# Level 64 of a triangular inverse: the z projection ahead of its first product, and its transposes and two products on 64x64 blocks of TensorE

## The chip, the cores and the metric

The kernel runs on one core of one Trainium2 chip. A core has TensorE (matrix products, "PE"; its weight loads "PEld"), VectorE ("DVE"), ScalarE ("ACT"), GpSimd ("POOL") and SyncE ("SP", which issues the DMAs here). The metric is the device time of one execution in microseconds; lower is better. All data are 32-bit floats. The engines run on their own instruction streams and wait for one another by semaphores.

## What is computed

The program is two transformer layers on x of shape (2, 1024, 256). Each layer adds an attention part and a feed-forward part to x. The change touches only the attention part of the first layer, a gated delta rule with 16 key heads, 32 value heads and head size 128. Cut to what matters:

```python
qkvz = hidden_states @ W_qkvz            # per key head: q, k, two v, two z
...
y = silu(conv4(mixed))                   # causal convolution over time, 4 taps
q = l2norm(q) * DK ** -0.5 ; k = l2norm(k)
def step(S, inp):                        # one token
    qt, kt, vt, gt, bt = inp
    S = S * exp(gt)[:, None, None]
    kv = einsum('hk,hkv->hv', kt, S)
    delta = (vt - kv) * bt[:, None]
    S = S + kt[:, :, None] * delta[:, None, :]
    return S, einsum('hk,hkv->hv', qt, S)
...
gated = core * silu(z)
gated = gated * rsqrt(mean(gated * gated) + EPS) * norm_w
return gated.reshape(B, Tn, VDIM) @ W_out
```

## The kernel before, in words

The tokens are handled in chunks of 128. Within a chunk the recurrence turns into matrix products with the inverse T of a unit triangular 128x128 matrix that is built from N (the decayed products of the keys); W is T transposed. One step of the long loop is one chunk of one key head, for both batches and both value heads, so each operation has U = 4 matrices side by side. There are 16 heads x 8 chunks = 128 steps (`STEPS`). The loop is a software pipeline: `body(s)` of every engine runs its functions on steps of different lag (`S_P`, `S_S`, `S_F`, `S_L`, `S_D`, `S_E` = 0, 1, 2, 5, 6, 7 steps back). The order of work on an engine is the order of the calls in its `body`; nothing reorders it. It is written out 16 times and looped (`pipeline`).

T is built in levels. GpSimd inverts the 16x16 blocks of the diagonal by rows (`base_first`, `base_rest`: once for two chunks, so that every second step has more GpSimd work), and SyncE carries them through DRAM into `Tm` and `Wm` (`base_out`, `dump`). TensorE and VectorE then join the blocks to 64x64 (`x16`, `w1`, `w2`, `w3` on TensorE; `xev16` and `add_k` on VectorE). The last level, 64, joins the two 64x64 halves:

- `t64` (L572): four transposes of W give T; `tev64` (ScalarE, L869) copies their upper left quarters from bank 5 to `Tm`.
- `x64` (L583): four products of N by the left half of T, into bank 5; `xev64` (ScalarE, L878) copies them negated to `Xs64`, whose right half stays zero.
- `w64` (L593): four products of `Xs64` by the right half of W into bank 4; `add_w64` (VectorE, L941) copies the upper 64 partitions into the upper right quarter of W. `solve` (L681) uses W in the next step.

All three are issued as 128-row products, though only one 64x64 quarter of each matters. A 32-bit product of one matrix shows as two matmul records, a transpose as one.

Around them stand in a step of TensorE: `state_in` (L513), `x16` (L528), `front` (L606, L611, L617), `solve` (L681), `w1` (L541), `apply` (L692, L695), `values` (L630), `w2` (L551), `project` (L651), `w3` (L561), `project` (L651), `t64`, `gated_tp` (L706: transposes of the gated output), `x64`, `zproj` (L668: x by the z weights, into bank 1), `w64`, `project_out` (L721: into bank 0). ScalarE copies gated_tp's result (`gtev`, L888) between `tev64` and `xev64`. VectorE's `accumulate` (L950) adds project_out's result to x. A tile's shape on the array follows from rows x columns of the weights; the profile writes it as 128*128.

Of the kernel before, what the change touches and what calls it, by code (L numbers as in the profile page):

```python
# [8 lines left out]
ACT = mybir.ActivationFunctionType  # L9
AX = mybir.AxisListType  # L10

P = 128
B, T, D = 2, 1024, 256
# [5 lines left out]
U = 4  # L19
# [89 lines left out]
def delta_rule(nc, ins, m, acc, xn, xnT, gates):  # L109
# [5 lines left out]
    RING = 4  # L115

    with ExitStack() as ctx:
# [30 lines left out]
        mkX = sb("mkX", [P, P])  # L148
        Xs = sb("Xs", [P, U, P])
        Wk = [sb(f"Wk{r}", [P, U, P]) for r in range(2)]  # L150
        Xs64 = sb("Xs64", [P, U, P])
        S = sb("S", [P, U, P])
        R = sb("R", [P, U, P])
        Us = sb("Us", [P, U, P])
# [72 lines left out]
        def wait(eng, sem, val):  # L227
            if not (isinstance(val, int) and val <= 0):
                eng.wait_ge(sem, val)
# [13 lines left out]
        with nc.Block() as block:  # L243
# [93 lines left out]
            @block.gpsimd  # L337
            def _(pool):
                pool.memset(conv[0][:], 0.0).then_inc(setup, 1)
                for tile in (S, Xs64):  # L340
                    pool.memset(tile[:], 0.0)
                pool.memset(mhalf[:], -0.5)
                pool.memset(mkX[:], -1.0)
                pool.wait_ge(m["made"], 2)
# [155 lines left out]
            def _(pe):  # L500
# [63 lines left out]
                def t64(s):  # L564

                    t = s.back(S_L)
                    if not t.live:
                        return
                    W = Wm[t.c // 2 % 2][:, t.c % 2]
                    wait(pe, w3_rdy, t.done())  # L570
                    for u in range(U):
                        i = pe.transpose(bU[5][:, u], W[:, u, :], m["ident"][:])  # L572
                    i.then_inc(t64_tp, 1)

                def x64(s):

                    t = s.back(S_L)
                    if not t.live:
                        return
                    T = Tm[t.c // 2 % 2][:, t.c % 2]  # L580
                    wait(pe, t64_rdy, t.done())
                    for u in range(U):
                        i = pe.matmul(bH[5][:, u], N[t.c % RING][:, u, :], T[:, u, 0:64], start=True, stop=True)  # L583
                    i.then_inc(x64_mm, 1)

                def w64(s):
                    t = s.back(S_L)
                    if not t.live:
                        return
                    W = Wm[t.c // 2 % 2][:, t.c % 2]  # L590
                    wait(pe, xs64_rdy, t.done())
                    for u in range(U):
                        i = pe.matmul(bH[4][:, u], Xs64[:, u, :], W[:, u, 64:], start=True, stop=True)  # L593
                    i.then_inc(w64_mm, 1)

                def front(s):
# [59 lines left out]
                def zproj(s):  # L656

                    t = s.back(S_L)
                    if not t.live:
                        return  # L660
                    pe.wait_ge(wz_in, t.head(16, 16))
                    wait(pe, araw_rdy, min(t.done(-S_L), STEPS) if t.i is None else t.done(-S_L))
                    ends(pe, s, exp_rdy, t, S_F - S_L)
                    ends(pe, s, zz_rdy, t, 1)
                    for b in range(B):
                        for k in range(KT):
                            n = 2 * t.c + b
                            i = pe.matmul(bB[1][:, b], xnT[:, k, n * P:(n + 1) * P], wz[:, k, :],  # L668
                                          start=(k == 0), stop=(k == KT - 1))
                    i.then_inc(z_mm, 1)  # L670
# [27 lines left out]
                def gated_tp(s):  # L698

                    t = s.back(S_E)  # L700
                    if not t.live:
                        return
                    pe.wait_ge(gatn_rdy, t.done())
                    wait(pe, o_rdy, min(t.done(-1), STEPS) if t.i is None else t.done(-1))
                    for u in range(U):
                        i = pe.transpose(bU[6][:, u], gatn[:, u, :], m["ident"][:])  # L706
                    i.then_inc(g_tp, 1)

                def project_out(s):

                    t = s.back(S_E)
                    if not t.live:
                        return
                    pe.wait_ge(gT_rdy, t.done())
                    wait(pe, wo_in, t.head(16, 16))
                    wait(pe, braw_rdy, min(t.done(-S_E), STEPS) if t.i is None else t.done(-S_E))
                    ends(pe, s, vb_rdy, t, S_F - S_E)
                    ends(pe, s, acc_rdy, t, 1)
                    for h in range(2):
                        for v in range(2):  # L720
                            i = pe.matmul(bB[0][:, h], gT[:, 2 * h + v, :], wout[:, v, :], start=(v == 0), stop=(v == 1))  # L721
                    i.then_inc(out_mm, 1)
# [15 lines left out]
                def body(s):  # L738
                    state_in(s)
                    x16(s)  # L740
                    front(s)
                    solve(s)
                    w1(s)
                    apply(s)
                    values(s)
                    w2(s)
                    project(s, 0)
                    w3(s)
                    project(s, 1)
                    t64(s)  # L750
                    gated_tp(s)
                    x64(s)
                    zproj(s)
                    w64(s)
                    project_out(s)
                    norm_tp(s)
                pipeline(pe, body)

# [1 line left out]
            def _(act):  # L760
# [102 lines left out]
                def tev64(s):  # L863

                    t = s.back(S_L)
                    if not t.live:
                        return
                    act.wait_ge(t64_tp, t.done())
                    act.activation(Tm[t.c // 2 % 2][0:64, t.c % 2, :, 0:64], bU[5][0:64, :, 0:64],  # L869
                                   ACT.Copy).then_inc(t64_rdy, 1)  # L870

                def xev64(s):

                    t = s.back(S_L)
                    if not t.live:
                        return
                    act.wait_ge(x64_mm, t.done())
                    act.activation(Xs64[:, :, 0:64], bH[5], ACT.Copy, scale=-1.0).then_inc(xs64_rdy, 1)  # L878

                def gtev(s):  # L880

# [49 lines left out]
            def _(dve):  # L931
# [174 lines left out]
                                                 op1=ALU.add).then_inc(done[k], 1)  # L1106

                def body(s):
                    add_w64(s)
                    accumulate(s)  # L1110
                    rhs(s)
                    gate(s)
                    xev16(s)
                    silu(s)
                    uscale(s)
                    add_k(s, w1_mm, 4, Wk[0], w1_rdy)
                    strict(s)
                    update(s)
                    add_k(s, w2_mm, 5, Wk[1], w2_rdy)
                    output(s)  # L1120
                    add_k(s, w3_mm, 4, None, w3_rdy)
                    attention(s)
                    taps(s, 0)
                    taps(s, 1)
                    norm_apply(s)
                    norm_stats(s)
# [1189 lines left out]
```

## Time and profile before

| | |
|---|---|
| median of 3 runs | 3441.93 us (3438.68 to 3442.51) |
| the profiled execution | 3440.38 us, span of its instructions 3438.6 us |
| mean granted clock of TensorE | 0.985 of full speed |
| TensorE busy (records) | 3221.5 us, 94% |
| TensorE weight loads | 2551.1 us, 74% |
| VectorE / ScalarE / GpSimd busy | 2445.4 / 1811.7 / 1655.8 us |
| the long loop | from about 374 to 3100 us |

A busy record of TensorE includes the time in which it runs through the array, so that records of neighbours overlap; how long a group holds the engine is read from start to start. PEld rows are the weight loads, which can run beside the products before them. In rows of instructions in order of time, brackets at the end give the idle time of the engine before and what ended it; x8 means eight records merged into one row that starts with the first.

### The profile page before, as it was taken

Reading aid. Unit: us, or ns where it says so; the run is one execution under the profiler, and the core shown is the slowest. Engines: PE = TensorE matmul, PEld = TensorE weight load, DVE = VectorE, ACT = ScalarE, POOL = GpSimd, SP = SyncE. Lnnn points to the kernel's source line nnn. Section 1 sums busy time; section 2 is a strip of 40 time slices with the busy share of each in tenths; the row PEclk is TensorE's granted clock in tenths of the full one; section 3 lists DMA queues with packets and bytes.
Section 4 is the critical chain, followed back from the end, with each engine's and each line's share of the span. In section 5 each row is a group of like instructions: output and inputs, shape, how many; then the busy total and the mean of one; then the engine's idle time right before and its main releaser. Section 6 shows DMA issues by size and latency. Waiting matters only on the chain. (4 is left out here: it accounts for less than half of the span.)

```text
span 3438.6 us, 60049 instructions
## 1 busy us (share of the span) xinstructions
PE 3221.5 (94%) x18409; PEld 2551.1 (74%) x18409; DVE 2445.4 (71%) x4675; ACT 1811.7 (53%) x5914; POOL 1655.8 (48%) x3745
## 2 busy tenths in 40 slices
PE   6997799999999999999999999999999999987998
PEld 4554588888877878887888788878877877874665
DVE  3433577777777777777777777777777777754776
ACT  4222465655555555555555555655555556542332
POOL 1001556656655565555566565656555656630000
PEclk9998899999999999999999999999999999998999
DMA  3000222121212121212121212121212121211000
GB/s 71 0 1 22 51 49 52 46 52 45 52 46 52 45 52 46 52 45 53 46 52 45 53 46 52 45 53 46 52 46 53 46 52 46 50 34 37 7 7 13
DMA packets 444985, 146.85 MB, mean 43 GB/s; under 512 B 217376, under 2 KB 443792, under 8 KB 444624
## 3 DMA queue, kind: packets, MB, share of 16 engines
q1 hardware_dynamic: 444624, 142.53, 16.9%
q8 instruction: 166, 2.72, 0.3%
q14 instruction: 195, 1.60, 0.2%
HBM read 97.40 MB, written 45.09 MB: 41 GB/s over the span
## 5 line engine op out<-in xcount | busy, mean ns | idle before, releaser
L1104 DVE SCALAR_TENSOR_TENSOR conv<-raw,ckq,conv 128x512 f32<-128x512 f32 x384 | 337.0, 890 | 24.7 <-ACT conv L860 15.6
L1104 DVE SCALAR_TENSOR_TENSOR conv<-raw,cv,conv 128x512 f32<-128x512 f32 x384 | 307.5, 815 | 9.1
L381 POOL TENSOR_SCALAR ty<-ty 128x4 f32<-128x4 f32 x128 | 34.7, 271 | 570.8 <-issue 455.2
L824 ACT ACTIVATE kd<-bank,gs 128x128 f32<-128x128 f32 x512 | 146.4, 369 | 284.8 <-PE bank L692 284.8
L455 POOL TENSOR_TENSOR Tb<-Tb,btmp 64x14 f32<-64x14 f32 (+6 forms) x896 | 258.2, 288 | 70.9 <-POOL btmp L451 1.2
L900 ACT ACTIVATE gatn<-gat,ty 128x128 f32<-128x128 f32 x512 | 163.6, 390 | 239.9 <-POOL ty L430 239.7
L451 POOL TENSOR_TENSOR btmp<-Bk,Tb 64x14 f32<-64x14 f32 (+6 forms) x896 | 252.0, 281 | 65.6
L859 ACT ACTIVATE raw<-bank 128x512 f32<-128x512 f32 x256 | 153.1, 598 | 236.4 <-PE bank L651 236.2
L651 PE MATMUL bank<-xnT,wkq 128*128 128x512 f32 x512 | 247.5, 608 | 12.7 <-DMA ckq<-in_L_attn_conv_w_dram 10.9
L721 PE MATMUL bank<-wout_h,gT 128*128 128x256 f32 x1024 | 249.2, 387 | 3.0 <-ACT gT L888 3.0
L668 PE MATMUL bank<-wz_h,xnT 128*128 128x256 f32 x1024 | 249.1, 386 | 0.0
L513 PE MATMUL bank<-S,ykq 128*128 128x256 f32 x1024 | 242.7, 380 | 4.4 <-issue 4.4
L651 PE MATMUL bank<-xnT,wv 128*128 128x512 f32 x512 | 242.2, 597 | 3.7 <-issue 3.7
L422 POOL TENSOR_TENSOR ty<-ty 128x4 f32<-128x4 f32 x128 | 74.5, 582 | 345.3 <-ACT sq_gat L847 345.3
L794 ACT ACTIVATE oq<-bank,gs 128x128 f32<-128x128 f32 x512 | 144.7, 364 | 162.0 <-PE bank L513 162.0
L513 PEld LDWEIGHTS bank<-S,ykq 128*128 128x128 f32 x1024 | 194.1, 190 | 32.2 <-issue 6.7
L583 PE MATMUL bank<-Tm,N 128*128 128x64 f32 x1024 | 141.5, 281 | 80.4 <-ACT Tm L869 80.3
L950 DVE TENSOR_TENSOR x<-x,bank 128x512 f32<-128x512 f32 x128 | 88.0, 688 | 169.3 <-PE bank L721 169.1
L583 PEld LDWEIGHTS bank<-Tm,N 128*128 128x128 f32 x1024 | 123.9, 191 | 111.0 <-ACT Tm L869 111.0
L721 PEld LDWEIGHTS bank<-wout_h,gT 128*128 128x128 f32 x1024 | 185.1, 191 | 22.9 <-ACT gT L888 3.4
L1050 DVE SCALAR_TENSOR_TENSOR N<-ET,ty,bank 128x128 f32<-128x128 f32 x512 | 144.3, 343 | 80.4 <-POOL ET L397 80.1
L668 PEld LDWEIGHTS bank<-wz_h,xnT 128*128 128x128 f32 x1024 | 185.1, 191 | 19.5
(348 smaller groups left out, 8506.0 us busy)
## 6 DMA issues: line engine op xcount, KB each, us to landing
blk_n<-N SPq DMA_DIRECT2D x128, 256.0 KB, 2.7
Tm<-blk_t SPq DMA_DIRECT2D x64, 512.0 KB, 4.2
Wm<-blk_w SPq DMA_DIRECT2D x64, 512.0 KB, 5.2
wkq<-in_L_attn_W_qkvz_dram SPq DMA_DIRECT2D x32, 128.0 KB, 2.3
wv<-in_L_attn_W_qkvz_dram SPq DMA_DIRECT2D x16, 256.0 KB
Bk<-blk_n SPq DMA_DIRECT2D x64, 64.0 KB, 2.7
blk_t<-Tb SPq DMA_DIRECT2D x64, 64.0 KB, 2.5
blk_w<-Wb SPq DMA_DIRECT2D x64, 64.0 KB, 2.5
```

The lines of the kernel that those rows point to most:

```text
L451: pool.tensor_tensor(tmp, Bk[:, j, j + 1:].unsqueeze(2).broadcast_to([64, 15 - j, j]), Tb[:, j, 0:j].unsqueeze(1).broadcast_to([64, 15 - j ...
L455: pool.tensor_tensor(Tb[:, j + 1:, 0:j], Tb[:, j + 1:, 0:j], tmp, ALU.subtract).then_inc(row_rdy, 1)
L513: i = pe.matmul(bB[6 + j][:, b], chunk(kq_of(t), t, j, b), S[:, 2 * b:2 * b + 2, :].rearrange("p v n -> p (v n)"), start=True, stop=True)
L583: i = pe.matmul(bH[5][:, u], N[t.c % RING][:, u, :], T[:, u, 0:64], start=True, stop=True)
L651: i = pe.matmul(bank[1 - j][:], w[:, k, j * P:(j + 1) * P], xnT[:, k, q * 512:(q + 1) * 512].rearrange("p (c b n) -> p b c n", c=2, b=B), ...
L668: i = pe.matmul(bB[1][:, b], xnT[:, k, n * P:(n + 1) * P], wz[:, k, :], start=(k == 0), stop=(k == KT - 1))
L721: i = pe.matmul(bB[0][:, h], gT[:, 2 * h + v, :], wout[:, v, :], start=(v == 0), stop=(v == 1))
L794: i = act.activation(oq[:, u, :], bU[7][:, u], ACT.Copy, scale=gs[t.c][:, GAM, u:u + 1])
L824: i = act.activation(kd[t.c % RING][:, u, :], bU[2][:, u // 2], ACT.Copy, scale=gs[t.c][:, DEC, u:u + 1])
L859: act.activation(raw[h][:, j, :, 3:], bB[1 - j], ACT.Copy)
L900: i = act.activation(gatn[:, u, :], gat[:, u, :], ACT.Copy, scale=ty[t.c][:, SC, u:u + 1])
L1104: dve.scalar_tensor_tensor(out=conv[h][:, j], in0=raw[h][:, j, :, k:k + 256], scalar=cw[:, j, k:k + 1], in1=conv[h][:, j], op0=ALU.mult, o ...
```

## The change

`zproj` is called before `x64`, and `w64` after `project_out`. The transposes take the upper left 64x64 quarter of W with a 64x64 identity, and put it into 64 partitions of bank 5. `x64` contracts over rows 0 to 63 only and computes the 64 columns that matter, into partitions 64 to 127 of bank 5. `w64` contracts over rows 64 to 127, into partitions 0 to 63 of bank 4. `Xs64` shrinks to its left half and isn't cleared any more. On VectorE `accumulate` moves ahead of `add_w64`. Three waits on `made`, a semaphore that has reached its value before the loop, come in ahead of the three groups.

```diff
--- before.py
+++ after.py
@@ -148,7 +148,7 @@
         mkX = sb("mkX", [P, P])
         Xs = sb("Xs", [P, U, P])
         Wk = [sb(f"Wk{r}", [P, U, P]) for r in range(2)]
-        Xs64 = sb("Xs64", [P, U, P])
+        Xs64 = sb("Xs64", [P, U, 64])
         S = sb("S", [P, U, P])
         R = sb("R", [P, U, P])
         Us = sb("Us", [P, U, P])
@@ -337,8 +337,7 @@
             @block.gpsimd
             def _(pool):
                 pool.memset(conv[0][:], 0.0).then_inc(setup, 1)
-                for tile in (S, Xs64):
-                    pool.memset(tile[:], 0.0)
+                pool.memset(S[:], 0.0)
                 pool.memset(mhalf[:], -0.5)
                 pool.memset(mkX[:], -1.0)
                 pool.wait_ge(m["made"], 2)
@@ -567,9 +566,11 @@
                     if not t.live:
                         return
                     W = Wm[t.c // 2 % 2][:, t.c % 2]
-                    wait(pe, w3_rdy, t.done())
+                    done = held(pe, t.done())
+                    pe.wait_ge(m["made"], 2)
+                    wait(pe, w3_rdy, done)
                     for u in range(U):
-                        i = pe.transpose(bU[5][:, u], W[:, u, :], m["ident"][:])
+                        i = pe.transpose(bH[5][0:64, u], W[0:64, u, 0:64], m["ident"][0:64, 0:64])
                     i.then_inc(t64_tp, 1)
 
                 def x64(s):
@@ -578,9 +579,11 @@
                     if not t.live:
                         return
                     T = Tm[t.c // 2 % 2][:, t.c % 2]
-                    wait(pe, t64_rdy, t.done())
+                    done = held(pe, t.done())
+                    pe.wait_ge(m["made"], 2)
+                    wait(pe, t64_rdy, done)
                     for u in range(U):
-                        i = pe.matmul(bH[5][:, u], N[t.c % RING][:, u, :], T[:, u, 0:64], start=True, stop=True)
+                        i = pe.matmul(bH[5][64:, u], N[t.c % RING][0:64, u, 64:], T[0:64, u, 0:64], start=True, stop=True)
                     i.then_inc(x64_mm, 1)
 
                 def w64(s):
@@ -588,9 +591,11 @@
                     if not t.live:
                         return
                     W = Wm[t.c // 2 % 2][:, t.c % 2]
-                    wait(pe, xs64_rdy, t.done())
+                    done = held(pe, t.done())
+                    pe.wait_ge(m["made"], 2)
+                    wait(pe, xs64_rdy, done)
                     for u in range(U):
-                        i = pe.matmul(bH[4][:, u], Xs64[:, u, :], W[:, u, 64:], start=True, stop=True)
+                        i = pe.matmul(bH[4][0:64, u], Xs64[64:, u, :], W[64:, u, 64:], start=True, stop=True)
                     i.then_inc(w64_mm, 1)
 
                 def front(s):
@@ -749,10 +754,10 @@
                     project(s, 1)
                     t64(s)
                     gated_tp(s)
+                    zproj(s)
                     x64(s)
-                    zproj(s)
+                    project_out(s)
                     w64(s)
-                    project_out(s)
                     norm_tp(s)
                 pipeline(pe, body)
 
@@ -866,7 +871,7 @@
                     if not t.live:
                         return
                     act.wait_ge(t64_tp, t.done())
-                    act.activation(Tm[t.c // 2 % 2][0:64, t.c % 2, :, 0:64], bU[5][0:64, :, 0:64],
+                    act.activation(Tm[t.c // 2 % 2][0:64, t.c % 2, :, 0:64], bH[5][0:64],
                                    ACT.Copy).then_inc(t64_rdy, 1)
 
                 def xev64(s):
@@ -875,7 +880,7 @@
                     if not t.live:
                         return
                     act.wait_ge(x64_mm, t.done())
-                    act.activation(Xs64[:, :, 0:64], bH[5], ACT.Copy, scale=-1.0).then_inc(xs64_rdy, 1)
+                    act.activation(Xs64[64:], bH[5][64:], ACT.Copy, scale=-1.0).then_inc(xs64_rdy, 1)
 
                 def gtev(s):
 
@@ -1106,8 +1111,8 @@
                                                  op1=ALU.add).then_inc(done[k], 1)
 
                 def body(s):
+                    accumulate(s)
                     add_w64(s)
-                    accumulate(s)
                     rhs(s)
                     gate(s)
                     xev16(s)
```

Line numbers of the changed kernel are moved by up to five. Two places show how the order of instructions moves. The first is TensorE at the end of a step of the long loop, before the change (Wm and Tm are W and T, bank is PSUM, gatn the gated output):

```order
L572 MATMUL bank<-ident,Wm 128x128 x4
L706 MATMUL bank<-ident,gatn 128x128 x4
L583 MATMUL bank<-Tm,N 128x64 x4
L229 REGISTER_ALU
L668 MATMUL bank<-wz_h,xnT 128x256 x4
L593 MATMUL bank<-Wm,Xs 128x64 x4
L721 MATMUL bank<-wout_h,gT 128x256 x4
L513 MATMUL bank<-S,ykq 128x256 x4
```

and after it:

```order
L573 MATMUL bank<-ident,Wm 64x64 x4
L711 MATMUL bank<-ident,gatn 128x128 x4
L229 REGISTER_ALU
L673 MATMUL bank<-wz_h,xnT 128x256 x4
L586 MATMUL bank<-Tm,N 64x64 x4
L726 MATMUL bank<-wout_h,gT 128x256 x4
L598 MATMUL bank<-Wm,Xs 64x64 x4
L512 MATMUL bank<-S,ykq 128x256 x4
```

The z projection (`wz_h`) now follows the transposes of the gated output directly, level 64's first product stands between it and the output projection (`wout_h`), the second one after both; the three groups of level 64 have 64 rows and columns.

The second is VectorE at the turn from one step to the next, before the change (conv: the last taps of the convolution; x: the running sum; R: the right-hand side for `solve`):

```order
L1104 SCALAR_TENSOR_TENSOR conv<-raw,ckq,conv 128x512 x6
L941 COPY Wm<-bank 64x4x64
L950 TENSOR_TENSOR x<-x,bank 128x512
L986 SCALAR_TENSOR_TENSOR R<-bank,gs,vb 128x128 x4
L996 SCALAR_TENSOR_TENSOR zz<-zz,bank 128x512
```

and after it:

```order
L1109 SCALAR_TENSOR_TENSOR conv<-raw,ckq,conv 128x512 x6
L955 TENSOR_TENSOR x<-x,bank 128x512
L946 COPY Wm<-bank 64x4x64
L991 SCALAR_TENSOR_TENSOR R<-bank,gs,vb 128x128 x4
L1001 SCALAR_TENSOR_TENSOR zz<-zz,bank 128x512
```

The copy into W and the addition to x have changed places; the right-hand side follows both as before.

## Rows read from the trace of the kernel before

**Rows 1.** Busy time of each engine in a window: PE, PEld, DVE, ACT, POOL, then TensorE's clock.
```profile
core 0: us, PE busy (x) PEld busy (x) DVE busy (x) ACT busy (x) POOL busy (x), PEclk, DMA share, GB/s
1000.00:1500.00 500.00, 483.17 (x2952) 399.26 (x2951) 386.65 (x728) 298.11 (x1013) 298.14 (x665) 1.00 0.21 50
```

**Rows 2.** List of waits, 400 to 3070 us: total us, times, longest.
```profile
PE bank L583 <- ACT Tm L869: 79.2, 122, 1.1
```

**Rows 3.** Instructions in order of time, one step: start, duration, engine, line; TensorE.
```profile
1501.70 1.89 PE L513 MATMUL bank<-S,ykq 128*128 128x256 f32 x8
...
1515.86 0.60 PE L572 MATMUL bank<-ident,Wm 128*128 128x128 f32 x4
...
1516.30 0.60 PE L706 MATMUL bank<-ident,gatn 128*128 128x128 f32 x4
...
1517.55 0.97 PEld L583 LDWEIGHTS bank<-Tm,N 128*128 128x128 f32 x8 [0.89 <-ACT Tm L869]
1517.55 1.11 PE L583 MATMUL bank<-Tm,N 128*128 128x64 f32 x8 [0.65 <-ACT Tm L869]
...
1518.49 1.95 PE L668 MATMUL bank<-wz_h,xnT 128*128 128x256 f32 x8
...
1520.27 1.00 PE L593 MATMUL bank<-Wm,Xs 128*128 128x64 f32 x8
...
1521.11 1.95 PE L721 MATMUL bank<-wout_h,gT 128*128 128x256 f32 x8
...
1522.89 1.89 PE L513 MATMUL bank<-S,ykq 128*128 128x256 f32 x8
```

**Rows 4.** In order of time: weight loads of the second layer, 3211.5 to 3214.4 us.
```profile
3212.00 0.29 PEld L1992 LDWEIGHTS t_O<-a_S,qBT 32*128 32x128 f32 x2 [0.76 <-issue]
3212.62 0.30 PEld L1994 LDWEIGHTS t_O<-xn,at 128*128 128x128 f32 x2 [0.33 <-issue]
3213.25 0.14 PEld L1995 LDWEIGHTS t_A<-xn,pk 128*32 128x32 f32 x2 [0.33 <-issue]
3213.80 0.30 PEld L1979 LDWEIGHTS t_U<-wu,xnT 128*128 128x128 f32 x2 [0.41 <-issue]
```

**Rows 5.** In order of time: weight loads on smaller tiles, two places.
```profile
32.01 0.57 PEld L1320 LDWEIGHTS tp<-ident,a 64*128 64x128 f32 x8 [0.17 <-ACT w2A L1404]
...
3126.42 1.31 PEld L1828 LDWEIGHTS psg<-ones,a_gfB 128*32 128x32 f32 x32 [0.65 <-issue]
```

**Rows 6.** In order of time: the way through GpSimd and ScalarE, two steps.
```profile
1506.24 0.23 POOL L381 TENSOR_SCALAR ty<-ty 128x4 f32<-128x4 f32 x1 [3.48 <-issue]
...
1522.29 0.20 POOL L430 TENSOR_TENSOR ty<-ty 128x4 f32<-128x4 f32 x1
1522.53 1.28 ACT L900 ACTIVATE gatn<-gat,ty 128x128 f32<-128x128 f32 x4 [3.46 <-POOL ty L430]
...
1526.15 0.28 ACT L804 ACTIVATE sq_kq<-bank 128x128 bf16<-128x128 f32 x1
...
1527.43 0.34 POOL L381 TENSOR_SCALAR ty<-ty 128x4 f32<-128x4 f32 x1 [4.94 <-issue]
...
1530.95 1.12 DVE L1050 SCALAR_TENSOR_TENSOR N<-ET,ty,bank 128x128 f32<-128x128 f32 x4 [0.61 <-POOL ET L397]
...
1533.03 0.68 DVE L1016 TENSOR_TENSOR Wk<-Wm,bank 128x512 f32<-128x512 f32 x1
...
1534.44 1.05 PE L561 MATMUL bank<-Wk,Xs 128*128 128x128 f32 x8
```

**Rows 7.** In order of time: VectorE at the start of a step.
```profile
1523.09 0.69 DVE L950 TENSOR_TENSOR x<-x,bank 128x512 f32<-128x512 f32 x1 [1.37 <-PE bank L721]
...
1523.96 1.12 DVE L986 SCALAR_TENSOR_TENSOR R<-bank,gs,vb 128x128 f32<-128x128 f32 x4 [0.18 <-PE bank L513]
```

**Rows 8.** The issue of Tm's load in order of time; then waits, 1000 to 1500 us.
```profile
1519.02 0.38 SPq L308 DMA_DIRECT2D Tm<-blk_t  x1
...
PEld bank L528 <- DMA Tm<-blk_t: 2.4, 4, 0.7
```

**Rows 9.** Instructions grouped by line and shape, the whole run.
```profile
L1963 PE MATMUL t_T<-ident,pk 128*32 128x128 f32 x16 | 4.5, 282 | 0.0
```

## The prediction

> **What bounds the kernel now.** I read the busy time by windows first. In the middle of the long loop TensorE is busy 483 of 500 us at a granted clock of 1.00, that is 2.4 GHz, VectorE 387, ScalarE and GpSimd 298 each [rows 1]. So the loop goes at TensorE's pace, and a change is worth what it takes from TensorE's row of work. The list of waits names where TensorE itself stands still: nearly all of it is one wait, 79.2 us in 122 of the 128 steps, ahead of the first product of level 64 (x64, L583), for ScalarE's copy of the transposed W (L869) [rows 2]. Then I read one step in order of time [rows 3]. It starts with state_in (L513) at 1501.70, the next one at 1522.89: 21.19 us. At its end stand t64 (L572), gated_tp (L706), the wait, x64 (L583), zproj (L668), w64 (L593), project_out (L721).
>
> What a group costs is the distance from its start to the next group's start. A 32-bit product is two records, a transpose one. L593, 8 records: 1521.11 - 1520.27 = 0.84 us, 0.105 to 0.11 each, although each streams only 64 columns; L572, 4 records with 128 columns: 0.44. The 8 loads of L583 lie 0.11 apart ((0.97 - 0.19) / 7) [rows 3]. So the two products of level 64 are paced by their 128-column loads, not by their streams. zproj takes 1.78 us for 8 records of 256 columns, 0.22 each.
>
> **The change, part by part.**
>
> *zproj ahead of x64.* Today gated_tp's streams end at 1516.30 + 0.44 = 1516.74 and zproj's begin at 1518.49: 1.75 us for x64 with its wait [rows 3]. zproj needs no semaphore that comes late (its bank was emptied by the first copy of `evac`), so it goes straight behind gated_tp, and its 1.78 us cover L869's copy, which is late by 0.65 only. The wait goes. What is late next at this place: project_out's gT (its ScalarE copy, L888, stands ahead of xev64, and is done before x64 is), and w64's wait for the copy of x64's result, which project_out's 1.78 us cover.
>
> *Blocks of 64x64.* Two effects of opposite sign. Each record gets shorter: loads have 64 columns instead of 128, and streams have 64. No row shows a 64*64 tile. The nearest are L1320, transposes on a 64*128 tile with 64 columns streamed: 8 loads in 0.57 us with 0.14 for one, 0.061 apart; and L1828, on a 128*32 tile with one column streamed: 32 loads in 1.31 us, 0.04 apart [rows 5]. So the pitch lies between 0.04 and today's 0.11; I take 0.06, the row with the same stream length.
>
> Against that, a change of tile shape costs. In the second layer L1992 (32*128), L1994 (128*128), L1995 (128*32) and L1979 (128*128) follow one another, each with two loads 0.11 (for the 32 columns 0.03) apart and, but for the last, two streams of 256 columns, 0.43 together by zproj's pitch. Their first loads start 0.62, 0.63 and 0.55 us apart [rows 4]. Taking off the stream and the first load leaves 0.08, 0.09 and 0.09 us: the first load of another shape starts only about 0.09 us after the last stream before it has ended, and then nothing hides this load. L1995 has no semaphore wait, so it is the shape. An excursion to 64*64 and back costs 0.09 + its first load (0.05; 0.03 in a transpose) + records x 0.06 + 0.09 + the first load of the next group (0.11; 0.05 if that is a transpose).
>
> The Trainium skill (TensorEngine Tiling (Array Packing), Key Properties) says that changing the tiling mode, not just the tile, drains TensorE; the trace agrees with its 0.09 us.
>
> Sum for one step: x64 0.09 + 0.05 + 0.48 + 0.09 + 0.11 = 0.82 in place of 1.75: gain 0.93. w64 0.82 in place of 0.84: gain 0.02. t64 0.09 + 0.03 + 0.24 + 0.09 + 0.05 = 0.50 in place of 0.44: loss 0.06. Together 0.89 us. So tiling by itself does nearly nothing for t64 and w64; the gain is the wait, and half of x64. With a pitch of 0.04 the three groups give 0.4 more (1.29), with 0.11 they give -0.11 to -0.26 (below).
>
> The Trainium skill (TensorE: Matmul & The Clock Gate, "What overlaps and what doesn't") says that a load overlaps a running matmul only if its row group differs. Here all records of a group share one. By that rule a record would take load plus stream, 0.055 + 0.055 = 0.11. The trace speaks against it: on L1320's tile load and stream in turn would be about 0.11 too, and its pitch is 0.061; on whole arrays 0.22, and L583 shows 0.11. It is the third rival.
>
> *Order on VectorE.* `accumulate` now precedes `add_w64`. Today L950 waits for project_out, starts at 1523.09 (0.20 after the next state_in) and the right-hand side L986 at 1523.96, which waits for state_in [rows 7]. project_out now ends 0.82 earlier relative to state_in, so L950 runs at about -0.6 to +0.1, the copy of w64's result (0.41 us) at about +0.1 to +0.5, both before L986's +1.07. Nothing. If that cover were gone, solve (L681) is still over 4 us away.
>
> *The rest.* ScalarE's copy of x64's result has half the partitions and stays a copy of 256 columns; GpSimd's shorter clearing of Xs64 is once per program; three further waits on a semaphore long reached cost nothing I can find a row for. Nothing for all of these.
>
> **What is late next.** With 0.89 us off a step, covers elsewhere shrink by 0.89. Every second step GpSimd holds the rest of the base inverse and is occupied from L381 (1506.24) up to L430 (1522.49, when ScalarE starts L900); then ScalarE works without a gap through L900, tanh, zz and oq to the norms L804 at 1526.15, then GpSimd's L381 at 1527.43, the mask of ET, VectorE's L1050 at 1530.95 and L1016, 1533.03 to 1533.71, on which w3 (L561) waits [rows 6]. This path hangs on the step before, not on TensorE's start of this one. L561 streams at 1534.44 today; 0.89 earlier is 1533.55. The path lets it start at 1533.71 + 0.05 + a load of 0.11 = 1533.87. So in each pair of steps 0.32 of 1.78 us comes back as a wait of w3.
>
> Second, the load of Tm. It is issued at 1519.02 and feeds L528; in 500 us, some 12 pairs, L528's loads already wait for it 4 times, up to 0.7 us [rows 8]. In these the 0.89 are lost, of which 0.32 would have been lost at w3 anyhow: 0.57 in every third pair, 0.19 per pair. The pair gains 1.78 - 0.32 - 0.19 = 1.27 us. For the 122 steps with the wait [rows 2], 61 pairs: 78 us. The profiled execution took 3440.4 us for a span of 3438.6, and the median is 3441.9; from the median, **3364 us**, -2.3%.
>
> **The rivals.**
> First, all covers hold: w3 and Tm are ready in time. For it: the gaps are within what a reordering of ScalarE and GpSimd may give. Against: ScalarE's row from L900 to L804 has no slack. 122 x 0.89 = 109 us: 3333.
> Second, the late path costs its whole 0.89 in every second step, as the load of Tm or the ScalarE path would do if they had no slack now. Gain 0.89 per pair, 54 us: 3388. Against: w3 has 0.5 us between 1533.87 and 1534.44.
> Third, the slower side: records on 64x64 blocks are no closer than 0.11 us. Place: L572, L583, L593, 20 records a step. x64 then takes 0.09 + 0.11 + 0.88 + 0.09 + 0.11 = 1.28, w64 the same, t64 0.72: gains 0.47, -0.44, -0.28, together -0.25; times 122 is +31 us: 3473. It turns to a loss when the pitch is above 0.06 + 0.89 / 20 = 0.105. Against it are rows 5.
> Fourth, no change: a switch to a 64x64 tile costs not 0.09 but 0.24 us. Six a step are 0.9 us more and eat the gain: 3442. Against: three switches between other shapes agree on 0.09.
> The change may also not do what it says in one point: the transposes on a 64-column tile. The Trainium skill (the tiling page, Restrictions) says that column tiling excludes the 32-bit transpose mode; then t64 would be 8 records, 0.24 us a step more, 29 us. L1963 transposes to a 128*32 tile with 16 records for 16 calls, 282 ns each, like others [rows 9]: the trace disagrees.
>
> **How the numbers follow.** Forecast 0.50, first rival 0.20, second 0.13, third 0.10, fourth 0.07. A measurement of this kernel can tell some 0.2% (7 us) from no change. Faster takes the forecast and the first two, 0.83; same 0.07; slower 0.10. The range takes in the first two rivals with a few us on either side, for a pitch a little under 0.06 and for switches of 0.12: 3326 to 3412. It leaves out the third and fourth, 0.17.
>
> **What would show it.** In the changed profile: no wait of L586 for ScalarE's Tm; zproj's stream directly behind gated_tp's; loads of the 64*64 records 0.06 apart; a gap of 0.09 us before each first load of another shape, six a step; the distance from state_in to state_in about 20.3 us in one step and 20.6 in the other; new waits of L560 for VectorE's Wk in every second step, and longer ones of L527 for the DMA of Tm. I am wrong if the pitch is near 0.11, if the switches cost more than 0.2 us, or if a wait appears in both steps of a pair.

## The result, and the profile after

The changed kernel takes 3365.5 us (median of 4 runs, 3364.2 to 3366.6), the kernel before 3440.7 us beside it; the ratio is 0.978, 95% interval 0.977 to 0.980. The profiled execution has a span of 3363.0 us in place of 3438.6, so 75.6 us less.

The busy time of each engine in the middle of the long loop, columns as in [rows 1]:

```profile
1000.00:1500.00 500.00, 493.92 (x3048) 383.36 (x3046) 395.91 (x758) 308.94 (x1046) 306.86 (x685) 1.00 0.21 51
```

TensorE is busy 494 of 500 us instead of 483; the same work now passes in less time. The list of waits of the changed kernel, 400 to 3000 us (waiting engine, tile and line, releaser; total us, times, longest), answers to [rows 2]:

```profile
PEld bank L560 <- DVE Wk L1021: 42.6, 66, 1.0
PEld bank L586 <- issue: 41.8, 126, 0.3
...
PE bank L622 <- DVE zz L1001: 17.1, 54, 0.3
...
PE bank L512 <- issue: 13.0, 6, 2.4
...
PE bank L527 <- DMA Tm<-blk_t: 2.0, 3, 1.2
```

The wait of x64 (now L586) for ScalarE is gone. Three things stand in its place. TensorE's weight loads at w3 (L560) wait for VectorE in every second step. L622 in `front` waits for VectorE's zz in nearly every second step. And six times state_in (L512) starts up to 2.4 us late with "issue" as the reason, that is, the profile shows nothing that it waited for. One step of TensorE in order of time (start, duration, engine, line) answers to [rows 3]:

```profile
1506.08 1.99 PE L512 MATMUL bank<-S,ykq 128*128 128x256 f32 x8
...
1520.44 0.25 PEld L573 LDWEIGHTS bank<-ident,Wm 64*64 64x64 f32 x4 [0.76 <-issue]
...
1520.78 0.42 PEld L711 LDWEIGHTS bank<-ident,gatn 128*128 128x128 f32 x4
...
1521.27 1.89 PE L673 MATMUL bank<-wz_h,xnT 128*128 128x256 f32 x8
...
1523.09 0.54 PEld L586 LDWEIGHTS bank<-Tm,N 64*64 64x64 f32 x8 [0.33 <-issue]
...
1523.70 1.59 PEld L726 LDWEIGHTS bank<-wout_h,gT 128*128 128x128 f32 x8
...
1525.62 0.54 PEld L598 LDWEIGHTS bank<-Wm,Xs 64*64 64x64 f32 x8 [0.33 <-issue]
...
1526.23 1.99 PE L512 MATMUL bank<-S,ykq 128*128 128x256 f32 x8
```

From state_in to state_in it is 20.15 us instead of 21.19. Read the new tile here: the 8 loads of L586 take 0.54 us in all, and one lasts 0.135, so they lie (0.54 - 0.135) / 7 = 0.058 us apart. zproj's streams begin at 1521.27; the group lasts 1.89 us, one record 0.38, so the records lie (1.89 - 0.38) / 7 = 0.216 us apart, and the 8 streams end 1.73 us later, at 1523.00. L586's first load starts at 1523.09, 0.09 later. From there to the first load of L726 it is 0.61: load 0.05, streams 0.47, gap 0.09. So x64 holds the array for 0.09 + 0.61 + the load of L726 0.11 = 0.81 us, against a forecast of 0.82. The Trainium skill's rule that a change of tiling mode drains TensorE (TensorEngine Tiling (Array Packing), Key Properties) now has its number for 64*64 in this trace, 0.09 us each way. The Trainium skill's other rule, that loads overlap a running product only in another row group (TensorE: Matmul & The Clock Gate, "What overlaps and what doesn't"), does not hold in it: 0.058 us is load or stream, not their sum. The transposes on the 64*64 tile (L573) are four records for four calls, not eight.

The step behind it takes longer, 20.91 us. The rows show the path that sets it (ty, ET, N and Wk are tiles on this path, gatn the gated output):

```profile
1527.02 1.28 ACT L905 ACTIVATE gatn<-gat,ty 128x128 f32<-128x128 f32 x4 [2.83 <-POOL ty L429]
...
1530.73 1.10 PE L622 MATMUL bank<-gtri,gt 128*128 128x512 f32 x2 [0.32 <-DVE zz L1001]
1530.76 0.30 ACT L809 ACTIVATE sq_kq<-bank 128x128 bf16<-128x128 f32 x1
...
1532.08 0.33 POOL L380 TENSOR_SCALAR ty<-ty 128x4 f32<-128x4 f32 x1 [5.10 <-issue]
...
1535.59 1.26 DVE L1055 SCALAR_TENSOR_TENSOR N<-ET,ty,bank 128x128 f32<-128x128 f32 x4 [1.25 <-POOL ET L396]
...
1537.80 0.68 DVE L1021 TENSOR_TENSOR Wk<-Wm,bank 128x512 f32<-128x512 f32 x1
...
1538.54 1.16 PE L560 MATMUL bank<-Wk,Xs 128*128 128x128 f32 x8
...
1547.14 0.48 PE L512 MATMUL bank<-S,ykq 128*128 128x256 f32 x1
```

This is the path of [rows 6], stage by stage: ScalarE from normed (L905) to the norms (L809), GpSimd, N (L1055), Wk (L1021), w3 (L560), which now starts the moment Wk is there. L622 stands still on the way. Over all ordinary steps, read from the starts of state_in, the short one is 20.15 us and the long one 20.67 to 20.91, mostly 20.77: a pair takes 40.92 us, before it took 42.38. (The pair shown stands shortly ahead of a turn of the loop and has one of the longest steps.)

Once in 16 steps the program's loop turns back, and there the changed kernel loses. The first 16 steps stand ahead of the loop and the other 112 are seven passes through it, so it turns back six times; these are the six waits of L512 in the list. After the turn at 1588, the weight loads of w64 and state_in, and the busy time with the granted clock (last but two):

```profile
1587.45 0.54 PEld L598 LDWEIGHTS bank<-Wm,Xs 64*64 64x64 f32 x8 [0.33 <-issue]
1590.44 3.06 PEld L512 LDWEIGHTS bank<-S,ykq 128*128 128x128 f32 x8 [2.45 <-issue]
```

```profile
1588.00:1590.50 2.50, 0.18 (x4) 0.06 (x1) 1.01 (x2) 1.65 (x2) 1.80 (x7) 0.99 0.02 7
1590.50:1592.00 1.50, 1.50 (x4) 1.23 (x5) 0.00 (x0) 0.00 (x0) 0.00 (x0) 0.50 0.07 16
1592.00:1593.50 1.50, 1.50 (x5) 1.23 (x4) 0.86 (x4) 0.00 (x0) 0.00 (x0) 0.50 0.02 5
...
1595.00:1600.00 5.00, 5.00 (x36) 4.34 (x35) 3.21 (x4) 2.02 (x11) 3.00 (x7) 1.00 0.01 3
```

TensorE loads nothing for 2.45 us, and then works at a granted clock of 0.50, that is 1.2 of 2.4 GHz, for a little over 3 us: state_in's loads take 3.06 us instead of 1.59. All six turns of this run show such a drop. In the kernel before, the same place shows a shorter gap and no drop, at any of its six turns:

```profile
1629.00:1630.00 1.00, 0.40 (x3) 0.37 (x3) 0.69 (x1) 0.83 (x2) 0.75 (x3) 1.00 0.02 8
1630.00:1632.00 2.00, 2.00 (x14) 1.82 (x13) 1.14 (x5) 0.37 (x2) 0.00 (x0) 1.00 0.06 12
```

Counted over the two steps at this turn, the excess over an ordinary pair is 44.97 - 40.92 = 4.05 us after and 43.25 - 42.38 = 0.87 us before. Over the six turns it is 3.5 to 4.0 us each after, 22.7 in all, and 0.8 to 1.3 before, 5.9 in all: 16.8 more.

From the third state_in to the 122nd, 119 steps take 2532.05 us before (438.15 to 2970.20) and 2457.54 after (434.79 to 2892.33): 74.5 of the 75.6 us. The ordinary steps give 87 us and the turns take 16.8 of it. Another 4.4 come from the load of Tm: before, ten steps were 0.2 to 0.6 us longer than 21.19 because of it, after, none away from the turns is.

### The profile page after: what moved, and what is told of

Its sections match the earlier page's. It is cut to its first block and busy times, and to the rows that moved or that the text cites. A ratio compares the mean times of both kernels' runs of the same rounds, so it can differ in the third digit from the quotient of the medians.

```text
span 3363.0 us, 60432 instructions
## 1 busy us (share of the span) xinstructions
PE 3199.9 (95%) x18409; PEld 2401.6 (71%) x18409; DVE 2429.9 (72%) x4675; ACT 1822.9 (54%) x5914; POOL 1661.3 (49%) x3744
## 5 line engine op out<-in xcount | busy, mean ns | idle before, releaser
L512 PE MATMUL bank<-S,ykq 128*128 128x256 f32 x1024 | 263.3, 401 | 13.0 <-issue 13.0
L905 ACT ACTIVATE gatn<-gat,ty 128x128 f32<-128x128 f32 x512 | 163.6, 390 | 178.2 <-POOL ty L429 176.5
L726 PE MATMUL bank<-wout_h,gT 128*128 128x256 f32 x1024 | 256.8, 394 | 3.0 <-ACT gT L893 3.0
L1055 DVE SCALAR_TENSOR_TENSOR N<-ET,ty,bank 128x128 f32<-128x128 f32 x512 | 144.3, 343 | 120.5 <-POOL ET L396 120.1
L512 PEld LDWEIGHTS bank<-S,ykq 128*128 128x128 f32 x1024 | 189.5, 195 | 43.8 <-issue 13.8
L991 DVE SCALAR_TENSOR_TENSOR R<-bank,gs,vb 128x128 f32<-128x128 f32 x512 | 144.1, 344 | 93.7 <-PE bank L512 93.7
L726 PEld LDWEIGHTS bank<-wout_h,gT 128*128 128x128 f32 x1024 | 185.0, 190 | 32.3 <-ACT gT L893 3.5
L1021 DVE TENSOR_TENSOR Wk<-Wm,bank 128x512 f32<-128x512 f32 x256 | 175.5, 686 | 31.0 <-PE bank L540 28.9
L560 PEld LDWEIGHTS bank<-Wk,Xs 128*128 128x128 f32 x1024 | 129.3, 191 | 72.3 <-DVE Wk L1021 42.8
```

What stands on the lines that cost most here:

```text
L512: i = pe.matmul(bB[6 + j][:, b], chunk(kq_of(t), t, j, b), S[:, 2 * b:2 * b + 2, :].rearrange("p v n -> p (v n)"), start=True, stop=True)
L905: i = act.activation(gatn[:, u, :], gat[:, u, :], ACT.Copy, scale=ty[t.c][:, SC, u:u + 1])
L1021: dve.tensor_tensor(W if into is None else into[:], W, bU[bk], ALU.add).then_inc(done, 1)
```

## The experiments

Each kernel was timed in rounds beside the kernel before (3441 us in all of them).

**The order alone.** The changed calls on TensorE and VectorE, all products on whole arrays.

```diff
--- before
@@ TensorE body
-                    x64(s)
                     zproj(s)
-                    w64(s)
+                    x64(s)
                     project_out(s)
+                    w64(s)
@@ VectorE body
+                    accumulate(s)
                     add_w64(s)
-                    accumulate(s)
```

> The changed order on TensorE and VectorE, with all products and transposes of level 64 on the whole array as before. My theory: the order gives nearly the whole gain, because the wait for ScalarE's Tm goes; x64 then takes 0.84 to 0.9 us as w64 does, which is 0.86 to 0.91 us less a step than the 1.75 of before; the late path to w3 takes some 0.5 back in every second step, and the seven turns of the long loop cost about 2 us more each. Sum 61 x 1.3 - 15 = 64 us less than before, about 3377 us. Rival: the blocks carry half of the gain; then this kernel stands near 3400 us.

Measured: 3358.8 us (3357.0 to 3360.3), ratio 0.976 (0.975 to 0.978). That is 7 us faster than the whole change, and 18 faster than I had written (which counted seven turns; there are six). The order carries all of the gain. Its end of a step and the late w3 of the long step, TensorE in order of time:

```profile
1521.99 1.89 PE L668 MATMUL bank<-wz_h,xnT 128*128 128x256 f32 x8
1523.71 1.00 PE L583 MATMUL bank<-Tm,N 128*128 128x64 f32 x8
1524.55 1.95 PE L721 MATMUL bank<-wout_h,gT 128*128 128x256 f32 x8
1526.34 1.00 PE L593 MATMUL bank<-Wm,Xs 128*128 128x64 f32 x8
1527.17 1.95 PE L513 MATMUL bank<-S,ykq 128*128 128x256 f32 x8
...
1539.15 1.16 PE L561 MATMUL bank<-Wk,Xs 128*128 128x128 f32 x8
```

x64 takes 0.84 us on the whole array and the step 20.28, only 0.13 more than with blocks; the long step is 20.61 instead of 20.77, so the pair is 40.89 against 40.92. What blocks save in the short step comes back in the long one, as a path that hangs on the step before would have it. Of the 4.6 us between the two profiled executions, 1.8 are these pairs and 2.1 the turns, where one of the six, the one in which the clock did not drop, took 42.95 us for its two steps and the others 44.3 to 44.9, against 44.4 to 45.0; the rest lies ahead of the steady steps and behind them.

**The blocks alone.** The changed kernel with the calls back in the order of before.

```diff
--- after
@@ TensorE body
-                    zproj(s)
                     x64(s)
-                    project_out(s)
+                    zproj(s)
                     w64(s)
+                    project_out(s)
@@ VectorE body
-                    accumulate(s)
                     add_w64(s)
+                    accumulate(s)
```

> The 64x64 blocks, in the order of before. My theory: x64 still waits for ScalarE's copy, which comes as late as before since ScalarE copies the projection first; x64 itself is 0.2 us shorter, the switches eat the rest; with 0.07 us that each of two groups behind a wide stream loses no more, 0.3 us a step, 128 steps: 37 us, about 3404 us. Turns of the loop as before (0.6 us of idle TensorE, no drop of its clock). Rival, the blocks do not pay at all or carry half of the 75 us: 3441, or under 3395 with shares that add up to no more than the whole.

Measured: 3411.7 us (3406.1 to 3416.1), ratio 0.992 (0.990 to 0.993), a little above the 3404 expected. The steps take 20.88 us, 0.31 less than before, as reckoned. The wait is all there:

```profile
PE bank L586 <- ACT Tm L874: 83.9, 122, 1.3
```

What I had wrong are the turns: their first step takes 22.1 to 22.7 us, where it took 21.9 to 22.4, and their second 21.4 to 22.0, where it took 21.3. Over the six turns that is 13.7 us above ordinary pairs instead of 5.9: 7.7 us, the size of the miss. The clock stays at 1.00 in all of them.

Blocks alone give 29 us, the order alone 82, both 75: they do not add. The path accounts for less than half of that. A pair of steps gains 1.49 us by the order, 0.63 by the blocks and 1.46 by both, 0.66 less than the sum. With the path out of the way (normed late, below; the blocks alone never meet it) the three are 1.82, 0.63 and 2.08, still 0.37 less. That part lies in TensorE's own row. In the old order x64 stands behind its wait and takes 0.94 us on the whole array, from start to start (L583 to L668 in [rows 3]), but 0.58 in blocks:

```profile
1522.30 0.65 PE L586 MATMUL bank<-Tm,N 64*64 64x64 f32 x8 [0.68 <-ACT Tm L874]
1522.88 1.99 PE L673 MATMUL bank<-wz_h,xnT 128*128 128x256 f32 x8
```

In the new order x64 on the whole array takes only 0.84, so there is less for the blocks to save.

**zz earlier on ScalarE.** In the changed kernel, `ztanh` ahead of `silu`.

```diff
@@ ScalarE body
-                    silu(s)
                     ztanh(s)
+                    silu(s)
```

> The changed kernel with two calls exchanged on ScalarE: ztanh ahead of silu, so that zz is ready 1.04 us earlier and TensorE's L622 need not wait for VectorE's zz in every second step. My theory: that wait lies inside the longer path ScalarE, GpSimd, VectorE to w3, whose length does not change, so w3 waits by as much more: 3365 us within 4, pair of steps 40.9 us. Rival: the wait at L622 is itself the price, 0.56 us in each of 61 pairs: 34 us less, 3331 us.

Measured: 3356.5 us (3351.9 to 3358.3), ratio 0.975 (0.974 to 0.976), 9 us under the changed kernel: near my side, but outside the 4 us that I had allowed. The waits of this kernel, 400 to 3000 us, no longer name L622; in its place w3 waits more often:

```profile
PEld bank L560 <- DVE Wk L1021: 68.9, 66, 1.2
...
PE bank L560 <- DVE Wk L1021: 17.8, 59, 0.8
```

The long step takes 20.68 us instead of 20.77, not 20.2. So the wait of 0.56 us at L622 lay inside the longer path but for 0.09 us. Those are 5.5 us in 61 pairs; two of the six turns, the ones in which the clock did not drop, were also over 1 us shorter than the others.

**Fewer turns of the loop.** The changed kernel, and the kernel before, with 32 steps written out.

```diff
-SLOTS = 16
+SLOTS = 32
```

> The changed kernel with 32 instead of 16 steps written out per turn of the long loop, so that 3 turns stand in place of 7; nothing else differs. My theory: one turn costs about 4.1 us here (TensorE stands still for 2.3 us, then goes at half its clock for some 3 us), so 4 turns less give 16 us: 3349 us. Rival: the long steps come from the loads of the next heads' weights, not from the turn; then they stay, and the time is 3365 us.

> The kernel before with 32 steps written out per turn. My theory: there a turn costs only about 0.8 us (0.6 us of idle TensorE, no lower clock), so 4 turns less give 3 us: 3438 us, against 14 us in the changed kernel. The part of the change that makes turns dearer is the last wait of a step, on the copy of x64's result: it passed 3.8 us ahead of the next step before, and 2.1 us now. Rival: a turn costs 4 us whatever the order; then 3425 us.

Measured: changed 3351.2 us (3349.1 to 3353.5), ratio 0.974 (0.973 to 0.975), 14.3 us less for 4 turns fewer (two in place of six). The kernel before: 3435.2 us (3432.8 to 3436.0), ratio 0.998 (0.997 to 0.999), 5.8 us less. Dividing by four does not give the price of a turn, because the waits for the load of Tm change as well. In the changed kernel the two turns that are left cost 3.9 us each, and six steps elsewhere are 0.4 to 1.7 us longer, 5.2 in all, because the load of Tm comes late:

```profile
PE bank L527 <- DMA Tm<-blk_t: 8.1, 8, 2.0
```

In the kernel before, the two that are left cost 1.0 and 1.3 us, and the steps with that wait go from 4.4 us in all to 1.8. So the turn costs time in both, some 3.8 us against 1.0; about a third of the 5.8 us is Tm. That the position of the last wait of a step is the reason fits the gaps, but the runs do not show it apart: the kernel with blocks in the old order has turns dearer than before, too.

**normed one slot later.** In the changed kernel, and in the order alone, ScalarE scales the gated output behind `expo` of the next slot.

```diff
@@ normed
-                    t = s.back(S_D)
+                    t = s.back(S_E)
@@ ScalarE body
                     expo(s)
+                    normed(s)
                     kdec(s)
...
                     xev64(s)
-                    normed(s)
```

> The changed kernel with ScalarE's normed (four copies, 1.28 us, whose result TensorE needs only near the end of the step) called one slot later, behind expo, where ScalarE waits 2.3 us for TensorE. My theory: what holds every second step at 20.77 us, while the other takes 20.15, is the path GpSimd's out_scale, normed, silu, zz, oq, norms, GpSimd's derive, ET, VectorE, w3; normed leaves it, the path gets 1.28 us shorter, and both steps take 20.15: 61 x 0.62 = 38 us less than the changed kernel, about 3327 us. Rival: the long step comes from the load of Tm or from VectorE's own row; then at most half of it goes, above 3345 us.

> The new order with whole-array products (as the order alone before) and normed one slot later. My theory: with the path away, both steps take 20.28 us, the pair 40.56 instead of 40.89: 3339 us; so the blocks, which were worth nothing with the path in place, are worth 0.13 us a step, 12 to 16 us between this kernel and the one with blocks and normed late. Rival: the blocks are worth nothing or cost time by themselves; then this kernel is no slower than that one.

Measured: with blocks 3330.9 us (3327.6 to 3333.1), ratio 0.968 (0.967 to 0.969); without 3341.4 us (3338.4 to 3341.6), ratio 0.971 (0.970 to 0.972). The long step is gone; state_in and w3 of the kernel with blocks, in order of time:

```profile
1509.05 1.99 PE L512 MATMUL bank<-S,ykq 128*128 128x256 f32 x8
1513.08 1.02 PE L622 MATMUL bank<-gtri,gt 128*128 128x512 f32 x2
1520.71 1.05 PE L560 MATMUL bank<-Wk,Xs 128*128 128x128 f32 x8
1529.21 1.99 PE L512 MATMUL bank<-S,ykq 128*128 128x256 f32 x8
1533.23 1.02 PE L622 MATMUL bank<-gtri,gt 128*128 128x512 f32 x2
1540.86 1.05 PE L560 MATMUL bank<-Wk,Xs 128*128 128x128 f32 x8
```

Every step away from the turns takes 20.15 us (20.28 without blocks), and neither L622 nor w3 waits there. The path was what held the long step. The gain is 34.6 us by the medians and 37.1 between the profiled executions, where I wrote 38. In the profiles the long steps give 37 us and the turns 4, and the end takes 4 back: 362.8 us from the last state_in on, instead of 358.9. With the path away, the blocks (and the three waits that come with them) are worth 10 us; with it in place they cost 7.

**normed later in the kernel before.** The same edit on the kernel before.

> The kernel before, with normed one slot later as in the changed one. My theory: there TensorE, not the path through ScalarE and GpSimd, sets every step (w3 stands 0.68 us behind the path), so a shorter path gives nothing: 3441 us within 5. Rival: normed late helps by itself, by freeing ScalarE ahead of the copy of Tm; then up to 30 us less.

Measured: 3442.2 us (3439.9 to 3445.3), ratio 1.0006 (0.9997 to 1.0015). Nothing, and the ordinary steps stay at 21.19 us, as the slack between the path and w3 in [rows 6] said. (I wrote 0.68 us for it; with w3's first load taken off it is 1534.44 - 1533.87 = 0.57.) Two smaller effects cancel in the total: the end of the loop takes 5.8 us longer, and only two steps instead of ten wait for Tm, 3.4 us less. In the order of before the path sets no step; it costs time only where the order has changed.

**The three further waits.** The order alone with normed late, plus the waits on a semaphore long reached.

```diff
+                    done = held(pe, t.done())
+                    pe.wait_ge(m["made"], 2)
-                    wait(pe, w3_rdy, t.done())
+                    wait(pe, w3_rdy, done)
...
```

> The new order on whole arrays with normed late (3341 us), plus the three waits on a semaphore long reached that the changed kernel has ahead of t64, x64 and w64. My theory: they cost nothing inside a step (20.28 us stay) and at most 0.3 us of idle TensorE at each of seven turns: 3341 to 3343 us. Rival: each takes time on TensorE's queue, 0.05 us or more; then 20 us more, 3360 us, and the blocks' own gain is larger than the 10 us that the two kernels with and without blocks show.

Measured: 3343.9 us (3340.3 to 3345.8), ratio 0.972 (0.970 to 0.973), against 3341.4 without. The ranges overlap, and the medians are 3 us apart, nothing like 20. Ordinary steps stay at 20.28 us, so the waits cost nothing there. At the turns they cost more than the 0.3 us I had allowed: where the clock did not drop, a turn's two steps are 1.9 to 2.4 us above an ordinary pair without them and 2.7 to 3.6 with them. In this profile the clock dropped at one turn of six, without the waits at two, which hides part of it.

**All together.** The changed kernel with normed late, 32 steps per turn, and the transposes of `t64` back on whole arrays.

```diff
-SLOTS = 16
+SLOTS = 32
...
-                        i = pe.transpose(bH[5][0:64, u], W[0:64, u, 0:64], m["ident"][0:64, 0:64])
+                        i = pe.transpose(bU[5][:, u], W[:, u, :], m["ident"][:])
...
+                    normed(s)
                     kdec(s)
```

> The changed kernel with normed late, 32 steps per turn, and t64 back on the whole array (its block form cost 0.50 in place of 0.44 us). My theory: 38 + 14 + 0.06 x 122 = 59 us less than the changed kernel: 3306 us. Rival: the load of Tm, which lands just in time, becomes the next wait in every second step as the steps get shorter: 3320 us or more.

Measured: 3315.5 us (3313.7 to 3319.4), ratio 0.964 (0.962 to 0.965): the fastest kernel of the study, 50 us under the changed one, 9 short of what I wrote. Its steps take 20.10 us, so `t64` is 0.05 cheaper on whole arrays. The rest lies in the wait that the rival named, though not in every second step:

```profile
PEld bank L527 <- DMA Tm<-blk_t: 13.9, 15, 2.5
...
PE bank L527 <- DMA Tm<-blk_t: 9.0, 7, 2.1
```

TensorE waits 9 us for the load of Tm, most of it in six steps that take 21.4 to 22.5 us. Shorter steps are not the reason that the rival gave: the kernel with normed late has steps of 20.15 us and waits 1.8 us for Tm, while the changed kernel with 32 steps per turn has its old step length and waits 8.1. In the changed kernel it comes with the 32 steps written out; why is not shown.

## Why the prediction was right, and where its terms were not

The forecast was 3364 us with a range of 3326 to 3412, and 3365.5 was measured. The mechanism is shown: the order removes the wait, the blocks pay little, and the path over ScalarE and GpSimd takes part back in every second step. But that the numbers lie 1.5 us apart is luck. Four terms were off by 16 to 18 us each, two in each direction: the step (18 more gain), the path (18 less), the load of Tm (16 more) and the turns (17 less).

- *The wait and x64.* x64 was sized at 0.82 us and takes 0.81; w64 0.82 and 0.81; t64 0.50, measured from the end of the projection's streams (1520.34) to the start of gated_tp's (1520.83), 0.49. Right.
- *The sum of a step.* Forecast 0.89, measured 21.19 - 20.15 = 1.04. The failed term is the length of the two wide groups. I took 1.78 us for zproj and project_out from start to start. That is what they take behind whole-array groups with streams of 64 columns, and I charged their first load behind the blocks on top of it. Behind transposes zproj takes 1.72 us, even with whole arrays, and behind blocks 1.73. So 0.05 to 0.06 us was counted double, twice; the last 0.03 are the three groups above.
- *The path to w3.* Forecast a loss of 0.32 us per pair; measured 0.62. With 1.04 instead of 0.89 TensorE reaches w3 earlier by 0.15, and the path itself is another 0.15 longer than I reckoned in the usual pair, 0.29 in the pair shown (w3 streams 32.46 us after the earlier state_in, where I had 32.17). ScalarE takes 3.74 us from L905 to L809, not 3.62, and L1055 1.26 instead of 1.12.
- *A wait not named.* L622 writes the bank that z was in, so it waits for VectorE's zz, on the same path. I had listed what ScalarE's row feeds only at its end. It cost little, as the experiment with zz earlier shows.
- *The load of Tm.* Forecast a loss of 0.19 us per pair, 12 us in all; it gave 4.4 us instead. Of the 64 loads before, 52 landed within 4.0 to 4.6 us of their issue and 12 took 5.3 to 6.0. After, all land within 4.0 to 4.7. I had taken the waits of [rows 8] for a fixed distance that shorter steps run into; they came from the slow landings, and these are gone. Why they are gone is not shown.
- *The turn of the loop.* Not in the forecast at all: 3.5 to 4.0 us instead of 0.8 to 1.3, six times, 17 us. I never looked at the one place in 16 steps where the pattern breaks.
- *A sum among the rivals.* Against the third rival I wrote that on whole arrays load and stream in turn would be 0.22 us. For L583, with a load of 0.11 and a stream of half that, it is 0.165. The 0.11 that was measured speaks against either.

Per pair the forecast was 1.78 - 0.32 - 0.19 = 1.27 us; measured are 2.08 - 0.62 = 1.46, 89 us in 61 pairs, of which the turns take 17 and the waits for Tm give 4 back. Of the rivals, the first (all covers hold, 3333) is the kernel with normed late, 3330.9. The second (the late path costs its whole share in every second step) is out, as the path took 0.62 of 1.04. The third (records no closer than 0.11) and the fourth (switches of 0.24 us) are out by the rows of L586.

## What to carry to other kernels

When an edit shortens a step, list every engine's path that hangs on the step before and note its slack; the smallest slack, not the edit, sets the new step, and two edits that both draw on it do not add. They may not add for another reason as well: here the blocks were worth 0.31 us a step behind a wait and 0.13 without it. Smaller tiles on TensorE pay only where the group is long enough to carry two switches of 0.09 us and a first load that nothing hides. Here, by the steps of 20.28, 20.15 and 20.10 us, eight records gained an estimated 0.09 us and four transposes lost 0.05. Read an ordinary step and also the steps at the loop's turns, all of them: in the order alone two turns of one execution differ by 1.9 us.

## What the runs showed of the hardware that I had not expected

- After 2.45 us without a load at the turn of the loop the granted clock fell from 1.00 to 0.50 for the next 3 us, and was 1.00 again at 1595; with the gaps of before, 0.5 to 1.1 us, it stayed at 1.00 at all six turns.
- A longer gap did not always bring the drop. In the order alone with normed late, four turns of six had none, and their second step takes 20.32 us instead of 21.9, so the drop itself costs 1.6 us. State_in's loads at a turn without and with the drop:

```profile
1249.26 1.59 PEld L513 LDWEIGHTS bank<-S,ykq 128*128 128x128 f32 x8 [1.65 <-issue]
1576.39 3.06 PEld L513 LDWEIGHTS bank<-S,ykq 128*128 128x128 f32 x8 [2.27 <-issue]
```

  The length of the gap alone does not decide it: between products it was 1.99 us at another turn of this run without a drop, and 1.54 at a turn of the order alone with one.
- A turn costs 3.5 to 4.0 us in the changed kernel and 0.8 to 1.3 us in the kernel before, by the two steps at each of the six.
- A transpose of 128x128 and one of 64x64 differ little in a group of four: 0.44 us against 0.49 with the switches, and 20.10 against 20.15 us for the step.
